# A four-layer network on one core: four changes of order, in two routers, an attention's projections and an attention's main loop

## The chip, the core and the metric

The kernel runs on one core of a Trainium2 chip. A core has TensorE (PE in the profile; its weight loads are PEld), VectorE (DVE), ScalarE (ACT), GpSimd (POOL) and SyncE (SP, which here only issues transfers). Every engine runs its own queue of instructions in order; an instruction that needs another engine's result waits at a semaphore, and all behind it on that queue wait too. The metric is device time in microseconds (us); the table below gives it for three runs.

## What is computed

Four layers, each of an attention or a recurrence and a feed-forward part, with a residual and a layer norm after each, on x of 4 x 512 tokens with 128 features, all in float32:

```python
x = _layernorm(x + _L0_attn_ref(x, ...))   # window attention
x = _layernorm(x + _L0_ffn_ref(x, ...))    # 16 experts, router r0
x = _layernorm(x + _L1_attn_ref(x, ...))   # direction attention, a1
x = _layernorm(x + _L1_ffn_ref(x, ...))    # 8 experts with capacity, router r1
x = _layernorm(x + _L2_attn_ref(x, ...))   # rotary attention, 8 heads of 128, a2
x = _layernorm(x + _L2_ffn_ref(x, ...))    # rotary attention, 16 heads of 64, h2; 31 experts
x = _layernorm(x + _L3_attn_ref(x, ...))   # recurrence
x = _layernorm(x + _L3_ffn_ref(x, ...))    # 8 experts, router r3 with a hidden layer
```

The four parts that the change touches compute this (shortened):

```python
# a1: three query and key numbers a head, and their products with fixed directions
q3 = (x @ Wq.T).reshape(B, T, 8, 3); k3 = (x @ Wk.T).reshape(B, T, 8, 3)
scores = einsum('bhtd,bhsd->bhts', q3, k3) * scale + q_on_dir[..., :, None] * k_on_dir[..., None, :]
# r1: the two best of 8 experts for each token; a place in the expert's list; then
h = gelu(einsum('ecd,edh->ech', exp_batches, c_fc)); exp_out = einsum('ech,ehd->ecd', h, c_proj)
# h2: on xn = _rmsnorm(x, gamma1), 16 heads of 64
q = _rope(xn @ q_w + q_b); k = _rope(xn @ k_w + k_b)
attn = softmax(where(causal, q @ k.T * scale, -inf)); attn_out = (attn @ v) @ o_w + o_b + xn
# r3
logits = gelu(xf @ gw1 + gb1) @ gw2 + gb2; scores = softmax(logits); topk_w, topk_idx = top_k(scores, 2)
```

## The kernel before

The program is a sequence of blocks, with a barrier of all engines between them. Activations lie feature-major: 128 features on the partitions, 2048 tokens along them, handled as four batches (B) of 512 columns (T). In every block each engine's order is written out by hand, and each wait names a semaphore and a count. A float32 matmul runs as two passes over its columns; where speed is wanted, operands are split into a rounded high part and a low part (value minus high part), and three single-pass products replace one.

**The norm at the head of a block** (Norm, lines 200 to 257, and Head, 259 to 320). For each batch b, PE centres the sum, ACT squares it, PE takes the variance, ACT makes the inverse root by Ln and Exp, and DVE multiplies (line 254), which gives x_fm. PE's order in Head.tensor is centre(b), variance(b - 1); behind the step b = 3 it calls the next part's tensor_early. Head.vector calls the next part's vector(dve, b) behind each of DVE's steps.

**Attention a1** (DirectionFront, 2427; direction_scores, 2045). The query and key weights (three rows a head) are spread to two 128 x 256 matrices by two products (line 2458, banks 0 and 1), copied to w_wide by DVE at b = 2 (line 2466), and at b = 3 the query part is multiplied by a scale (line 2472, which releases the semaphore scaled). PE waits for scaled, then runs 16 projections of 128 x 512 (line 2084) over four banks. Each result is split in three bfloat16 parts by ACT (2099, 2107), DVE (2134, 2146) and POOL.

**Router r1** (capacity_router, 1280) and its experts (capacity_experts, 1385). DVE ranks 8 logits a token, thresholds, counts (with two PE products, line 1324), and writes for each token and choice the row of its slot (slots, line 1382). Meanwhile ACT rounds the eight experts' first weights (w1_hi, line 1338) and POOL subtracts (w1_lo, line 1311). After the barrier POOL issues 32 indirect transfers (line 1415) that scatter the token rows to the experts' lists, SP fetches the lists, and PE starts the experts.

**Attention h2** (rope_attention with heads = 2, 1568). There are 32 units, one for a batch and a pair of heads. A unit U has four steps, one for each tile q of 128 queries, in the order q = 3, 0, 2, 1 (512, 128, 384 and 256 key columns, as the mask is causal). A step K has two items, one a head; item j = 2K + h uses score bank j % 5. The item's way: scores and mask on PE (lines 1739, 1742), the negative maximum on DVE (1932), the exponential with row sums on ACT (1852), transposes on PE into the same bank (1749), and a copy of these to p_t, by DVE for head 0 (1941) and by ACT for head 1 (1862). Scores of item j wait until the copy of item j - 5 has freed the bank. PE works one step ahead: scores(K + 1), transposes of K's head 0, a piece of other work, transposes of head 1, another piece; the pieces (function between) are the projections of unit U + 2 and the product with the values, the spread of the sums and the out product (line 1790) of unit U - 1. DVE runs maximum(K + 1), both heads, then copy_t(K). Rotary embedding of unit U + 2 goes through a swap of rows by SP's transfers and products on POOL. Attention a2 is the same function with heads = 1.

**Router r3** (router, 1017, with a hidden layer). PE computes two hidden tiles for each batch (line 1076, two banks in turn), ACT applies Gelu (1105), and behind all eight PE computes logits for 16 tiles of 128 tokens, two products each, which are 64 passes of 8 columns (line 1081). Then DVE ranks them. ACT rounds x (line 703) behind the last Gelu and POOL subtracts (x_lo, line 708).

## Time and profile before

| | us |
|---|---|
| median of three runs | 1852.05 (1846.07 to 1853.19) |
| the profiled execution | 1846.22, with a span of 1844.4 |
| mean granted clock of PE | 0.914 of full speed |

| engine | busy us | share of the span |
|---|---|---|
| PE | 1554.3 | 84% |
| PEld | 1002.0 | 54% |
| DVE | 1031.4 | 56% |
| ACT | 1004.5 | 54% |
| POOL | 767.2 | 42% |

The span is from the first to the last instruction; the profiled execution's time lies 1.8 us above it. A line of the page's groups gives busy time, mean time of one instruction and the idle time of its engine just before it. The idle times tell who waited, not whether it cost anything: ACT's exponentials in h2 stand idle before them for 132.4 us in all and DVE's maxima for 118.3, while PE's scores there show 20.6. Whether a wait counts must be read from the timeline of its stage. PE's clock is granted at one of two levels, 1.0 (2.4 GHz) or 0.5 (1.2 GHz); a number between is a mean over the stretch.

### The profile page before, as it was taken

How to read it: one execution, taken by the hardware profiler on the slowest of the kernel's cores; microseconds unless marked ns; L12 is line 12 of the kernel's file. 1: busy time of each engine (PE TensorE's matmuls, PEld its weight loads, DVE VectorE, ACT ScalarE, POOL GpSimd, SP SyncE). 2: the span in 40 equal slices, each digit the busy share in tenths (PEclk: the TensorE clock that was granted, in tenths of full speed). 3: DMA queues.
4: the chain of work that ended last, by engine and by line, in shares of the span. 5: the costliest groups of instructions: out<-in, count | busy, mean ns of one | idle time of the engine just before them, and what ended most of it. 6: DMA issues, size and time to landing. Idle time of an engine off the chain costs nothing. (4 is left out here: it accounts for less than half of the span.)

```text
span 1844.4 us, 27071 instructions
## 1 busy us (share of the span) xinstructions
PE 1554.3 (84%) x8739; PEld 1002.0 (54%) x8756; DVE 1031.4 (56%) x2126; ACT 1004.5 (54%) x2164; POOL 767.2 (42%) x712
## 2 busy tenths in 40 slices
PE   5658978860877899999789999999989999868898
PEld 3337643330874566666445555555448886323685
DVE  5956675631213655555355555555548886662575
ACT  4324554550423455555556656565538887664686
POOL 1224530027352566666264555545324443022263
PEclk8979977975887999999899999999979999979799
DMA  1008210021223222222211111111027652000330
GB/s 41 1 14 183 62 82 23 1 95 42 80 61 114 45 61 58 58 58 58 70 46 46 36 47 38 44 43 39 24 62 266 228 209 95 1 0 21 123 122 25
DMA packets 62165, 125.50 MB, mean 68 GB/s; under 512 B 14354, under 2 KB 29571, under 8 KB 55532
## 3 DMA queue, kind: packets, MB, share of 16 engines
q1 hardware_dynamic: 59724, 119.57, 22.2%
q0 software_dynamic: 2304, 4.24, 0.7%
q8 instruction: 69, 1.13, 0.3%
q14 instruction: 68, 0.56, 0.1%
HBM read 79.39 MB, written 11.35 MB: 49 GB/s over the span
## 5 line engine op out<-in xcount | busy, mean ns | idle before, releaser
L1852 ACT ACTIVATE h_probs<-psum,h_nmax 128x512 f32<-128x512 f32 (+3 forms) x256 | 132.7, 523 | 132.4 <-DVE h_nmax L1932 77.8
L1932 DVE TENSOR_REDUCE h_nmax<-psum 128x1 f32<-128x512 f32 (+3 forms) x256 | 113.5, 486 | 118.3 <-PE psum L1742 118.3
L1667 POOL TENSOR_TENSOR h_swapped<-h_swapped,rope_tables 128x512 f32<-128x512 f32 x64 | 81.9, 1280 | 158.4 <-DMA h_swapped<-h_raw 158.4
L897 ACT ACTIVATE psum<-psum,f_b 128x512 f32<-128x512 f32 x200 | 131.8, 659 | 27.8 <-PE psum L857 27.8
L823 POOL TENSOR_TENSOR e_lo<-e_gated,e_hi 128x512 fp32r<-128x512 f32 x59 | 76.1, 1290 | 148.1 <-ACT e_hi L909 148.1
L1852 ACT ACTIVATE a_probs<-psum,a_nmax 128x512 f32<-128x512 f32 (+3 forms) x128 | 67.6, 528 | 123.8 <-DVE a_nmax L1932 75.6
L1667 POOL TENSOR_TENSOR a_swapped<-a_swapped,a2f_a_tables 128x512 f32<-128x512 f32 x64 | 82.3, 1286 | 126.1 <-DMA a_swapped<-a_raw 125.9
L932 DVE TENSOR_TENSOR e_lo<-psum,e_hi 128x512 fp32r<-128x512 f32 x168 | 114.7, 683 | 26.4 <-ACT psum L897 26.4
L1739 PE MATMUL psum<-h_k,h_q 64*128 64x384 f32 (+3 forms) x512 | 104.9, 485 | 20.6 <-DVE h_p_t L1941 16.8
L855 PE MATMUL psum<-f_x_hi,f_w_hi 128*128 128x512 f32 x272 | 109.0, 401 | 5.8 <-DVE e_gated L946 3.9
L1749 PE MATMUL psum<-ident,h_probs 128*128 128x128 f32 x640 | 108.7, 277 | 0.4 <-ACT h_probs L1852 0.4
L856 PE MATMUL psum<-f_x_hi,f_w_lo 128*128 128x512 f32 x272 | 108.3, 398 | 0.0
L857 PE MATMUL psum<-f_x_lo,f_w_hi 128*128 128x512 f32 x272 | 108.1, 397 | 0.0
L1932 DVE TENSOR_REDUCE a_nmax<-psum 128x1 f32<-128x512 f32 (+3 forms) x128 | 62.4, 489 | 70.8 <-PE psum L1742 69.6
L1739 PE MATMUL psum<-a_k,a_q 128*128 128x512 f32 (+3 forms) x256 | 91.8, 441 | 6.4 <-DVE a_wvo L1924 6.4
L874 PE MATMUL psum<-e_lo,f_w_hi 128*128 128x512 f32 x236 | 92.8, 393 | 1.9 <-POOL e_lo L823 0.9
L871 PE MATMUL psum<-e_hi,f_w_hi 128*128 128x512 f32 x236 | 92.5, 392 | 0.0
L872 PE MATMUL psum<-e_hi,f_w_lo 128*128 128x512 f32 x236 | 92.4, 391 | 0.0
L1767 PE MATMUL psum<-h_p_t,h_v 128*64 128x256 f32 (+3 forms) x512 | 89.9, 451 | 0.0
L1739 PEld LDWEIGHTS psum<-h_k,h_q 64*128 64x128 f32 x512 | 40.0, 186 | 87.4 <-issue 49.4
L946 DVE TENSOR_TENSOR psum<-psum,e_gate 128x512 f32<-128x512 f32 x96 | 67.1, 699 | 33.4 <-ACT psum L897 29.0
L1749 PEld LDWEIGHTS psum<-ident,h_probs 128*128 128x128 f32 x640 | 72.0, 142 | 23.6 <-ACT h_probs L1852 19.2
(471 smaller groups left out, 4074.6 us busy)
## 6 DMA issues: line engine op xcount, KB each, us to landing
e_gate<-gates SPq DMA_DIRECT2D x39, 1024.0 KB, 4.8
a_swapped<-a_raw SPq DMA_DIRECT2D x128, 128.0 KB, 2.3
h_swapped<-h_raw SPq DMA_DIRECT2D x256, 64.0 KB, 2.0
e_gate<-gates SPq DMA_DIRECT2D x16, 512.0 KB, 7.4
f_w<-in_l_experts SPq DMA_DIRECT2D x17, 256.0 KB, 4.9
f_w<-in_l_experts SPq DMA_DIRECT2D x32, 128.0 KB, 4.7
slots<-a_empty SPq DMA_DIRECT2D x1, 2600.0 KB, 7.5
e_got<-slots SPq DMA_DIRECT2D x8, 325.0 KB, 5.5
```

The source lines that it names most:

```text
L855: nc.tensor.matmul(to, w_h, ex.x_hi[:, cols(b)], start=True, stop=False, skip_group_check=True)
L856: nc.tensor.matmul(to, w_l, ex.x_hi[:, cols(b)], start=False, stop=False, skip_group_check=True)
L857: nc.tensor.matmul(to, w_h, ex.x_lo[:, cols(b)], start=False, stop=True, skip_group_check=True).then_inc(hid_ready, 1)
L871: nc.tensor.matmul(to, w_h, hi[:, n % PLACES, :], start=start, stop=False, skip_group_check=True)
L874: nc.tensor.matmul(to, w_h, lo[:, n % PLACES, :], start=False, stop=True, skip_group_check=True).then_inc(out_done, 1)
L897: nc.scalar.activation(to, hidden_bank(n), ex.act_func, **bias(n)).then_inc(act_ready, 1)
L932: nc.vector.tensor_tensor(lo[:, n % PLACES, :], whole, hi[:, n % PLACES, :].bitcast(F32), ALU.subtract).then_inc(lo_dve, 1)
L1667: nc.gpsimd.tensor_tensor(swapped[:, j, :], swapped[:, j, :], tables[:, 2 * j + 1, :], ALU.mult).then_inc(sin_ready, 1)
L1739: nc.tensor.matmul(ring[j % RING][:, 0:(q + 1) * P], qs[rows, U % 3, q * P:(q + 1) * P], ks[rows, U % 3, 0:(q + 1) * P], start=True, stop= ...
L1749: last = nc.tensor.transpose(ring[j % RING][:, k * P:(k + 1) * P], probs[:, j % 4, k * P:(k + 1) * P], core.ident[:])
L1852: nc.scalar.activation(probs[:, j % 4, 0:(q + 1) * P], ring[j % RING][:, 0:(q + 1) * P], ACT.Exp, bias=nmax[:, j % 8:j % 8 + 1], accum_out ...
L1932: nc.vector.tensor_reduce(nmax[:, j % 8:j % 8 + 1], ring[j % RING][:, 0:(q + 1) * P], AX.X, ALU.max, negate=True).then_inc(max_ready, 1)
```

## The change

Four edits, none of which changes a value:

- r1: the low parts of the first weights are no longer subtracted by POOL in the router's block but by DVE at the start of the next block. PE waits for them (w1_split) before the first expert.
- r3: the logits of batch b - 1 are computed behind the hidden products of batch b; those of the last batch behind all.
- a1: tensor_early is called behind the step b = 1 of the norm on PE, and DVE's copies and scaling of the wide weights move from its steps 2 and 3 to its steps 0 and 1. Head is used by all blocks, but only a1 has a tensor_early.
- h2: at the last step of a unit (n = 3) DVE runs maximum(K + 1) for head 0, copy_t(K), then maximum(K + 1) for head 1. The end of the last unit, and a2, keep their order.

```diff
@@ Head.tensor
-            if b == B - 1:
+            if b == 1:
                 self.ahead.tensor_early(pe)
@@ router, tensor
+                def logits_of(b):
+                    pe.wait_ge(hid_ready, (b + 1) * KT)
+                    for t in range(b * QT, (b + 1) * QT):
+                        for k in range(KT):
+                            last = nc.tensor.matmul(logits[:, t, :], hid[:, k, t * P:(t + 1) * P], rw[:, k, :], start=k == 0, stop=k == KT - 1)
+                    return last
...
-                    pe.wait_ge(hid_ready, B * KT)
-                    for t in range(NT):
-                        for k in range(KT):
-                            last = nc.tensor.matmul(logits[:, t, :], hid[:, k, t * P:(t + 1) * P], rw[:, k, :], start=k == 0, stop=k == KT - 1)
-                    last.then_inc(logits_ready, 1)
+                        if b >= 1:
+                            logits_of(b - 1)
+                    logits_of(B - 1).then_inc(logits_ready, 1)
@@ capacity_router, gpsimd
-                for e in range(E):
-                    pool.wait_ge(w1_rounded, e + 1)
-                    nc.gpsimd.tensor_tensor(w1_lo[:, e, :], front.w1[:, e, :], w1_hi[:, e, :].bitcast(F32), ALU.subtract)
@@ capacity_experts, tensor
                 pe.wait_ge(front.w2_loaded, 16)
+                pe.wait_ge(w1_split, E)
@@ capacity_experts, vector
+                for e in range(E):
+                    nc.vector.tensor_tensor(w1_lo[:, e, :], front.w1[:, e, :], w1_hi[:, e, :].bitcast(F32), ALU.subtract).then_inc(w1_split, 1)
                 split_x(0)
@@ rope_attention, vector
-                def maximum(K):
+                def maximum(K, which=slice(None)):
...
-                    for j, h in step_items(K):
+                    for j, h in step_items(K)[which]:
...
-                    if K + 1 < steps:
+                    if K + 1 == steps:
+                        copy_t(K)
+                    elif heads == 2 and n == QT - 1:
+                        maximum(K + 1, slice(0, 1))
+                        copy_t(K)
+                        maximum(K + 1, slice(1, 2))
+                    else:
                         maximum(K + 1)
-                    copy_t(K)
+                        copy_t(K)
@@ DirectionFront.vector
-        if b == 2:
+        if b == 0:
...
-        if b == 3:
+        if b == 1:
```

DVE in h2, from the product that normalises a unit's values (h_y) on; h_nmax are the maxima, h_p_t the copies of transposed probabilities. Before:

```order
L1955 TENSOR_TENSOR h_y<-psum,h_r_sb 128x512
L1932 TENSOR_REDUCE h_nmax<-psum 128x1 x2
L1941 COPY h_p_t<-psum 128x2x128
L1932 TENSOR_REDUCE h_nmax<-psum 128x1 x2
L1941 COPY h_p_t<-psum 128x4x128
```

Now:

```order
L1960 TENSOR_TENSOR h_y<-psum,h_r_sb 128x512
L1937 TENSOR_REDUCE h_nmax<-psum 128x1
L1946 COPY h_p_t<-psum 128x2x128
L1937 TENSOR_REDUCE h_nmax<-psum 128x1 x3
L1946 COPY h_p_t<-psum 128x4x128
```

The copy of the last step (two tiles of 128) now stands between the two maxima of the next unit's first step; of the group of three, the first is the second head's and the other two belong to the step after.

PE at the start of a1, with the norm's centring (center_w) and variances (mean_w), the wide weights (a1w_spread) and the projections (a1w_w_wide). Before:

```order
L221 MATMUL psum<-sum_fm,center_w 128x512 x2
L241 MATMUL psum<-n0f__n0f_sq,mean_w 128x512
L221 MATMUL psum<-sum_fm,center_w 128x512
L241 MATMUL psum<-n0f__n0f_sq,mean_w 128x512
L221 MATMUL psum<-sum_fm,center_w 128x512
L241 MATMUL psum<-n0f__n0f_sq,mean_w 128x512
L2458 MATMUL psum<-a1w_spread,a1w_w 128x256 x2
L241 MATMUL psum<-n0f__n0f_sq,mean_w 128x512
L2084 MATMUL psum<-x_fm,a1w_w_wide 128x512 x4
```

Now:

```order
L221 MATMUL psum<-sum_fm,center_w 128x512 x2
L241 MATMUL psum<-n0f__n0f_sq,mean_w 128x512
L2469 MATMUL psum<-a1w_spread,a1w_w 128x256 x2
L221 MATMUL psum<-sum_fm,center_w 128x512
L241 MATMUL psum<-n0f__n0f_sq,mean_w 128x512
L221 MATMUL psum<-sum_fm,center_w 128x512
L241 MATMUL psum<-n0f__n0f_sq,mean_w 128x512 x2
L2095 MATMUL psum<-x_fm,a1w_w_wide 128x512 x4
```

The wide products moved from behind the third variance to behind the first, and nothing stands between the last variance and the projections.

PE in r3, with the hidden products (f_hw) and the logits (f_rw). Now (before it is one row of eight hidden products and one of 32 for the logits):

```order
L1083 MATMUL psum<-x_fm,f_hw 128x512 x4
L1071 MATMUL psum<-f_rw,r_hid 128x8 x8
L1083 MATMUL psum<-x_fm,f_hw 128x512 x2
L1071 MATMUL psum<-f_rw,r_hid 128x8 x8
L1083 MATMUL psum<-x_fm,f_hw 128x512 x2
L1071 MATMUL psum<-f_rw,r_hid 128x8 x16
```

Half of the logits now stand among the hidden products, half behind them.

## Rows read from the trace of the kernel before

**Rows 1.** Waits of 960 to 1320 us: waiter <- releaser: us, times, longest.
```profile
PE psum L1739 <- DVE h_p_t L1941: 12.8, 29, 0.4
```

**Rows 2.** Timeline in h2: start, length, engine, line, operation, count, [idle <-releaser].
```profile
1145.23 1.29 DVE L1932 TENSOR_REDUCE h_nmax<-psum 128x1 f32<-128x512 f32 x2 [0.26 <-PE psum L1742]
...
1145.53 1.02 PE L1790 MATMUL psum<-h_y,h2f_h_w 128*128 128x512 f32 x2
1146.01 0.69 ACT L1852 ACTIVATE h_probs<-psum,h_nmax 128x512 f32<-128x512 f32 x1 [1.82 <-issue]
1146.44 0.41 DVE L1941 COPY h_p_t<-psum 128x256 f32<-128x256 f32 x1
...
1147.00 0.49 PE L1739 MATMUL psum<-h_k,h_q 64*128 64x128 f32 x4 [0.44 <-DVE h_p_t L1941]
...
1147.54 0.61 PE L1749 MATMUL psum<-ident,h_probs 128*128 128x128 f32 x4
```

**Rows 3.** Timeline at the start of attention a1.
```profile
232.73 1.12 PE L2458 MATMUL psum<-a1w_spread,a1w_w 24*128 24x256 f32 x4
...
235.66 0.63 ACT L249 ACTIVATE n0f__n0f_rs<-n0f__n0f_rs 128x512 f32<-128x512 f32 x1
...
236.94 0.28 DVE L2472 TENSOR_SCALAR a1w_w_wide<-a1w_w_wide,a1w_scale 128x144 f32<-128x144 f32 x1
...
237.32 5.37 PE L2084 MATMUL psum<-x_fm,a1w_w_wide 128*128 128x512 f32 x8 [2.41 <-issue]
...
238.59 0.60 ACT L2099 ACTIVATE a1p_high<-psum 128x512 bf16<-128x512 f32 x1 [2.29 <-PE psum L2084]
...
243.42 3.60 PE L2084 MATMUL psum<-x_fm,a1w_w_wide 128*128 128x512 f32 x8
```

**Rows 4.** Groups by line and shape, 410 to 423 us: busy, mean ns, idle.
```profile
L1311 POOL TENSOR_TENSOR f_w_lo<-f_w,f_w_hi 128x512 fp32r<-128x512 f32 x8 | 10.1, 1300 | 1.4 <-ACT f_w_hi L1338 1.4
...
L1324 PE MATMUL psum<-r_chosen,f_counts 128*128 128x256 f32 x4 | 2.1, 674 | 6.7 <-DVE r_chosen L1363 6.7
...
L1379 DVE TENSOR_TENSOR r_upto<-r_upto,f_slot_base 128x256 f32<-128x256 f32 x1 | 1.4, 1367 | 0.0
L1363 DVE TENSOR_TENSOR r_chosen<-r_chosen 128x128 f32<-128x128 f32 x1 | 1.3, 1259 | 0.0
L1350 DVE TENSOR_SCALAR r_chosen<-r_marked 128x128 f32<-128x128 f32 x1 | 1.2, 1245 | 0.0
...
L1376 DVE SCALAR_TENSOR_TENSOR r_chosen<-r_upto,r_chosen 128x256 f32<-128x256 f32 x1 | 0.8, 833 | 0.0
L1380 DVE TENSOR_TENSOR r_upto<-r_upto,r_chosen 128x256 f32<-128x256 f32 x1 | 0.4, 424 | 0.0
```

**Rows 5.** Groups by line and shape in 422 to 467 us, the scatters.
```profile
L1415 POOL DMA_INDIRECT slots<-f_rows,f_slots x32 | 31.3, 980 | 12.0 <-issue 12.0
```

**Rows 6.** Line 1910: durations min/median/max ns, first and last start.
```profile
L1910 DVE TENSOR_TENSOR h_rot<-h_raw,rope_tables x32: 679/680/1662, 914.2 to 1307.0; 128x512 f32<-128x512 f32 x32
```

**Rows 7.** Timeline of router r3.
```profile
1695.04 5.89 PE L1076 MATMUL psum<-x_fm,f_hw 128*128 128x512 f32 x12 [1.81 <-ACT r_hid L1105]
...
1701.70 9.99 PE L1081 MATMUL psum<-f_rw,r_hid 128*128 128x8 f32 x64 [0.78 <-ACT r_hid L1105]
1702.25 4.95 POOL L708 TENSOR_TENSOR f_x_lo<-x_fm,f_x_hi 128x512 fp32r<-128x512 f32 x4 [7.96 <-ACT f_x_hi L703]
...
1711.80 0.29 DVE L1185 TENSOR_TENSOR r_scores<-psum,f_bias 128x128 f32<-128x128 f32 x1 [18.19 <-PE psum L1081]
...
1712.45 0.29 DVE L1187 TENSOR_TENSOR r_scores<-r_scores,r_small 128x128 f32<-128x128 f32 x1
```

**Rows 8.** Stretches: length, busy (count) PE PEld DVE ACT POOL, PEclk.
```profile
237.30:241.70 4.40, 4.38 (x7) 1.86 (x8) 1.58 (x3) 1.80 (x3) 0.00 (x0) 0.61 0.00 0
1701.70:1706.00 4.30, 4.30 (x39) 4.30 (x39) 0.00 (x0) 3.31 (x5) 3.75 (x4) 0.99 0.01 4
1706.00:1711.70 5.70, 5.69 (x28) 5.59 (x27) 0.00 (x0) 0.00 (x0) 1.19 (x1) 0.50 0.00 0
```

More of the change, by code:

```diff
@@ L1291, in capacity_router @@
         place = st.sb("place", [P, 2, NT])
-        (x_turned, first_rows, w1_rounded, shifted, exp_ready, chosen_ready, counted, dve_step) = (st.sem(n) for n in (
-            "x_turned", "first_rows", "w1_rounded", "shifted", "exp_ready", "chosen_ready", "counted", "dve_step"))
+        (x_turned, first_rows, shifted, exp_ready, chosen_ready, counted, dve_step) = (st.sem(n) for n in (
+            "x_turned", "first_rows", "shifted", "exp_ready", "chosen_ready", "counted", "dve_step"))
         within, totals = (core.psum[:, k, 0:2 * NT * E].rearrange("p (k t e) -> p k t e", k=2, e=E) for k in (1, 2))
@@ L1337, in _ @@
                     act.wait_ge(front.w1_loaded[e], 16)
-                    nc.scalar.activation(w1_hi[:, e, :], front.w1[:, e, :], ACT.Copy).then_inc(w1_rounded, 1)
+                    nc.scalar.activation(w1_hi[:, e, :], front.w1[:, e, :], ACT.Copy)
             @block.vector
@@ L1397, in capacity_experts @@
         hid = st.sb("hid", [P, 2, HT, CAPACITY])
-        (sent, turned, x_rounded, x_split, hid_psum, hid_ready, out_psum, out_ready, returned, joined) = (st.sem(n) for n in (
-            "sent", "turned", "x_rounded", "x_split", "hid_psum", "hid_ready", "out_psum", "out_ready", "returned", "joined"))
+        (w1_split, sent, turned, x_rounded, x_split, hid_psum, hid_ready, out_psum, out_ready, returned, joined) = (st.sem(n) for n in (
+            "w1_split", "sent", "turned", "x_rounded", "x_split", "hid_psum", "hid_ready", "out_psum", "out_ready", "returned", "joined"))
         got_loaded = [st.sem(f"got{e}_loaded") for e in range(E)]
```

## Prediction

> **What bounds the kernel now.** I read the page first: PE is busy 84% of the span, the other engines 42 to 56%, and the chain that ended last gives every line about 0%, so no single line bounds the program. Each stage has its own limit, and each edit must be priced in its own stage. I therefore read four stretches in the timeline: attention h2 (925 to 1341 us), the start of attention a1 (225 to 256), router r1 (393 to 468) and router r3 (1682 to 1723).
>
> In h2 a unit (one batch, two heads) takes about 12.9 us, 32 times, with PE nearly full. In the table of waits over 28 units the one true hole on PE is the 128-column scores waiting for DVE's copy of the transposed probabilities: 29 times, never over 0.4 us [rows 1]. The timeline shows its place. DVE starts the two 512-wide maxima at 1145.23, they take 1.29 us together, and only then, at 1146.44, comes the copy of step 3, head 0, which frees the bank that the next scores write. PE, whose last work was the two passes from 1145.53, starts those scores at 1147.00 [rows 2].
>
> In a1 PE builds the wide weights late, DVE scales them after the last norm step at 236.94, and PE's projections begin at 237.32; ACT's first split follows at 238.59 [rows 3]. In r1 DVE's small operations beside GpSimd's eight subtractions take up to 1.37 us where their like takes 0.42 [rows 4]. In r3 PE computes all hidden products first and then 64 passes for the logits in one block from 1701.70, and DVE waits for them until 1711.80 [rows 7]; in that block the granted clock is 0.99 (2.4 GHz) until 1706 and 0.50 (1.2 GHz) after [rows 8].
>
> **A copy between maxima (h2), the large term.** 31 times (the end of every unit but the last) DVE now runs max head 0, copy, max head 1. The two maxima take 1.29, so one occupies 0.65, and the copy can start near 1145.85 in place of 1146.44 and end near 1146.25; its transposes were issued ahead of 1145.53 and have ended. The scores started 0.15 after the copy's end, so they could now start at 1146.40. PE itself is free then: a 512-column fp32 pass takes its slot for 0.43 (eight of them 3.60, two 1.02, so (3.60 - 1.02)/6) [rows 2, 3], and two from 1145.53 end their slots at 1146.39. The gap between 1146.39 and 1147.00 is 0.61; the profile calls 0.44 of it a wait [rows 1, 2]. Some 0.1 between unlike groups of matmuls will stay, so I take 0.50: 31 x 0.50 = 15.5 us. The ends are 31 x 0.44 = 13.6 and 31 x 0.61 = 18.9.
>
> What is late next? PE's own order is scores, mask, transposes of head 0 at 1147.54, so 1147.0 after the change. They need the exponential that starts at 1146.01 and that the change does not move; with 0.69 for it and 0.1 for its accumulator it is done at 1146.8, 0.2 ahead [rows 2]. The second maximum is late by the copy's step, 0.41 less the usual overlap, about 0.33. The second exponential, bound by it, then ends near 1147.7; its transposes stand behind a projection of three passes and are wanted near 1148.2. ACT's copy behind it is also 0.3 later, in time for a bank that is reused over 1 us later. So the cost of 0.33 is covered by about 0.4 us, a thin cover, and it is paid in full if that is gone. POOL and the swap transfers work two units ahead and I charge nothing for them.
>
> **Wide weights in the norm's second step (a1).** The two products move from behind the third variance to behind the first. They take 1.12 us [rows 3] and PE is full there, so norm steps 1 to 3 move later; the last variance, held up by them today, then waits for its square instead. Walking the norm through ACT's order, the last exponential moves from 235.66 to about 236.0. Against that, DVE no longer scales after the last step, and PE goes from the last variance straight to the projections, at about 235.1 in place of 237.32. ACT's first split can start when its last exponential (0.63) is over, 236.75 in place of 238.59: 1.8 us gained. Today PE idles before it begins and gets a clock of 0.61 on average there [rows 8], so the first eight passes take 5.37 us, and eight a little later 3.60 [rows 3]. Without the hole the clock should stay at its upper level, which frees up to 1.8 us on PE; ACT, next in line and busy itself, lets through perhaps a third, 0.6. Sum 2.4, with ends 0 (another engine holds the stage) and 1.8 + 1.8 = 3.6 us. The weights' loads are issued by 226.7 and would have to land after 229.2 to add a wait.
>
> **Low parts off GpSimd (r1).** The eight subtractions leave POOL (10.1 us). Of DVE's operations beside them, the threshold L1350 falls from 1.25 to 0.29-0.42, the difference L1363 from 1.26 to 0.29 (the like in r3), L1376 from 0.83 to 0.42 and L1379 from 1.37 to 0.42 [rows 4, 7]: 0.9 + 1.0 + 0.4 + 0.9 = 3.2 us. L1365 and L1367 are slowed as well, but PE's two counting products (2.1 us) run beside them and DVE waits for these, so nothing comes of that. Slots, barrier and the 32 scatters move up by 3.2. The eight subtractions now stand first on DVE in the next block, ahead of split_x(0): 8 x 0.68 = 5.4 us by the 128x512 row with two SBUF operands [rows 6]. 32 scatters with 31.3 us of work and 12.0 of idle ahead of them hide them [rows 5], and PE's new wait for them is over long before the first gathered rows. What they do to POOL's scatters no row shows: at least 0; at most all of their 5.4. The nearest row: under DVE's interference POOL's eight subtractions still averaged 1.30 [rows 4], so POOL loses little and I take 0.5. Net gain 2.7, ends 3.2 and -2.2.
>
> The rule that speaks against this edit is in the Trainium skill, SBUF — State Buffer, section Who interferes with whom: a DVE instruction with two SBUF inputs contends with a GpSimd instruction that reads SBUF, and the second to issue blocks fully, but not with one that only writes. By that page the scatters, which read their offsets and data addresses, might be held for the whole of DVE's subtractions; the sum would then be 4.9 us worse, which is the fourth rival. No run here shows it.
>
> **Logits among the first products (r3).** Hidden products n2 to n7 run from 1695.04, each two passes of 0.43: 12 x 0.43 = 5.2 us. In the full-clock window 39 logits passes take 4.30 us, 0.11 each; in the half-clock one, 28 take 5.70, 0.20 each [rows 8]. Interleaved, PE has no hole: products of a batch, then the logits of the one before, whose Gelu is over by then. Ends: 1695.04 + 5.2 + 64 x 0.11 = 1707.3, if the clock stays up because full products stand between (the block began at full clock and kept it for over 4 us). DVE's first router operation was at 1711.80, 0.1 behind PE; it comes 4.4 us sooner. But Gelu ends 3 us later, so ACT's rounding and POOL's four x_lo subtractions (4.95) move from 1702.25 to about 1705.2-1710.2, now beside DVE's start. L1187 and L1191, with two SBUF operands, each wait for a POOL instruction: up to 1.0 together. Gain 3.5. The ends: at today's mean of 9.99/64 = 0.156 a pass it would be 1.5 - 1.0 = 0.5; without any blocking 4.4.
>
> **Sum.** 15.5 + 2.4 + 2.7 + 3.5 = 24.1 us. Against the profiled execution's own 1846.2 that is 1822.1. The median of the runs shown is 5.8 us above the profiled one, and I forecast a median: 1852.05 - 24.1 = 1828.
>
> **Rivals.** (1) h2 keeps half of its hole: the transposes of head 0 have only 0.2 us of margin, and semaphore latencies could eat 0.25 a unit. 24.1 - 7.8 = 16.3, 1836. (2) h2 gains nothing: the hole on PE appears elsewhere in the unit, since DVE's maxima mostly wait for PE's mask and ACT for DVE, a loop whose length the copy may not set. For it: these waits are there in the timeline; against: both engines wait because PE is late, and PE itself never stands long. Then 8.6 us, 1843.5. (3) Slower: DVE's queue becomes the loop. The copy waits for its transposes, and maximum head 1, its exponential and the transposes of head 1 queue behind that wait. It decides if the transposes end after 1146.6 instead of before 1146.0; the price is then about the whole copy and latencies, 1.0 a unit, +31 - 8.6 = +22 us, 1874. The order on PE speaks against it. (4) The scatters are held by DVE's subtractions: 4.9 worse, 1833.
>
> **How the numbers follow.** Forecast 0.62; rivals (1) 0.10, (2) 0.12, (3) 0.05, (4) 0.11. The bounds of the terms alone give gains from 11.9 (13.6 + 0 - 2.2 + 0.5) to 30.1 (18.9 + 3.6 + 3.2 + 4.4), that is 1840 to 1822 from the median; a measured median may also fall to the lowest of the runs shown, 6 us below, so the low end is 1816. The high end takes in rival (2): 1844. A measurement tells about 0.5% (9.3 us) from no change: below 1842.8 is faster. The forecast and rivals (1) and (4) lie there; rival (2) lies at the border, some of it on either side. Faster 0.84, same 0.11, slower 0.05.
>
> **What would show it.** h2: the 128-column scores start 0.1 us after PE's out product, no DVE wait ahead of them, and the unit is 12.4 us long; wrong if it is still 12.9. a1: first projection directly behind the last variance with clock 1.0, first split at 236.8. r1: first scatter 3.2 us sooner, then spacing as before; wrong if the first four are spread by 5 us. r3: logits passes of 0.11 throughout and DVE's start 4.4 us sooner. The forecast fails mainly if the h2 unit's length is not set by PE's queue.

## The result and the profile after

The changed kernel takes 1823.10 us (median of six runs, 1820.54 to 1829.45); the kernel before took 1852.24 on the same occasion. The ratio is 0.985, 95% interval 0.983 to 0.987, a gain of 28 us (25 to 31). The forecast was 1828, 24.1 us below the median of before. The profiled execution of the changed kernel took 1824.96 with a span of 1823.2. Its page gives each engine's busy time, share and instructions:

```profile
PE 1552.0 (85%) x8756; PEld 999.4 (55%) x8756; DVE 1033.2 (57%) x2134; ACT 1005.3 (55%) x2164; POOL 758.9 (42%) x704
```

PE is as busy as before within 2.3 us; what went is idle time between its products. GpSimd has 8.3 us less to do, and the eight subtractions take 4.9 us on DVE.

The span fell by only 21 us, since the profiled execution of before lies at the fast end of its kernel (1846.07 to 1853.78). One pair of profiles is therefore a poor witness for small terms: stages that no edit touches differ by up to 5 us between them (from h2's last maximum to the next norm 227.5 us before and 232.1 after). I use the pair for the mechanisms and all fourteen profiles of this study for the sizes (the table below).

**Attention h2.** The timeline of the changed kernel at the end of a unit (start, length, engine, line, operation, [idle before <- releaser]); it answers to [rows 2]:

```profile
1118.25 0.69 DVE L1937 TENSOR_REDUCE h_nmax<-psum 128x1 f32<-128x512 f32 x1 [0.27 <-PE psum L1747]
1118.85 0.41 DVE L1946 COPY h_p_t<-psum 128x256 f32<-128x256 f32 x1
1119.18 0.68 DVE L1937 TENSOR_REDUCE h_nmax<-psum 128x1 f32<-128x512 f32 x1
...
1119.02 0.69 ACT L1857 ACTIVATE h_probs<-psum,h_nmax 128x512 f32<-128x512 f32 x1 [1.82 <-issue]
...
1118.55 1.02 PE L1795 MATMUL psum<-h_y,h2f_h_w 128*128 128x512 f32 x2
1119.50 0.49 PE L1744 MATMUL psum<-h_k,h_q 64*128 64x128 f32 x4
...
1120.05 0.61 PE L1754 MATMUL psum<-ident,h_probs 128*128 128x128 f32 x4
```

The copy stands between the maxima. The scores follow PE's out product by 0.95 us from start to start, with no idle time recorded ahead of them; before it was 1.47 (1145.53 to 1147.00). The copy is over at 1119.26, 0.24 us before they start, so they no longer wait for it. In 950 to 1310 us the table of waits has no row for PE at all, where it had 12.8 us [rows 1], and the page's group of the scores shows what is left of their idle time, 7.5 us where before it was 20.6:

```profile
L1744 PE MATMUL psum<-h_k,h_q 64*128 64x384 f32 (+3 forms) x512 | 104.9, 486 | 7.5 <-POOL h_k L1677 5.0
```

From the first maximum of one unit to that of the next it is 12.38 us in 29 of the 31 spacings, where it was 12.90.

**Attention a1.** The start of the stage, whose first product begins at 227.61 (225.15 before); it answers to [rows 3], and the stretch under it to [rows 8] (length; busy and count of PE, PEld, DVE, ACT, POOL; granted clock; DMA share, GB/s):

```profile
236.77 1.12 PE L241 MATMUL psum<-n0f__n0f_sq,mean_w 128*128 128x512 f32 x2 [0.21 <-ACT n0f__n0f_sq L233]
...
237.33 0.63 ACT L249 ACTIVATE n0f__n0f_rs<-n0f__n0f_rs 128x512 f32<-128x512 f32 x1
...
237.74 3.60 PE L2095 MATMUL psum<-x_fm,a1w_w_wide 128*128 128x512 f32 x8
...
239.20 1.07 ACT L2110 ACTIVATE a1p_high<-psum 128x512 bf16<-128x512 f32 x2
```

```profile
235.00:240.00 5.00, 4.79 (x12) 1.94 (x11) 2.26 (x5) 4.90 (x9) 0.00 (x0) 1.00 0.00 0
```

The projections stand directly behind the last variance and run at 2.4 GHz, 3.60 us for eight passes in place of 5.37. Counted from the stage's first product, ACT's first split comes at 11.6 us in place of 13.4 (239.20 - 227.61; 238.59 - 225.15).

**Router r1.** Groups by line in 399 to 412 us (busy, mean ns | idle before), which answer to [rows 4], and the timeline of GpSimd behind them, to [rows 5]:

```profile
L1326 PE MATMUL psum<-r_chosen,f_counts 128*128 128x256 f32 x4 | 2.1, 674 | 5.7 <-DVE r_chosen L1365 5.7
...
L1373 DVE TENSOR_TENSOR_SCAN r_upto<-f_counts,psum 128x32 f32<-128x32 f32 x8 | 1.0, 200 | 1.6 <-PE psum L1326 1.6
...
L1378 DVE SCALAR_TENSOR_TENSOR r_chosen<-r_upto,r_chosen 128x256 f32<-128x256 f32 x1 | 0.4, 426 | 0.0
...
L1381 DVE TENSOR_TENSOR r_upto<-r_upto,f_slot_base 128x256 f32<-128x256 f32 x1 | 0.4, 425 | 0.0
...
L1365 DVE TENSOR_TENSOR r_chosen<-r_chosen 128x128 f32<-128x128 f32 x1 | 0.3, 293 | 0.0
```

```profile
412.03 1.53 POOL L1417 DMA_INDIRECT slots<-f_rows,f_slots  x1 [11.56 <-issue]
413.87 1.29 POOL L1417 DMA_INDIRECT slots<-f_rows,f_slots  x1 [0.30 <-issue]
415.47 1.50 POOL L1417 DMA_INDIRECT slots<-f_rows,f_slots  x1 [0.30 <-issue]
417.27 0.98 POOL L1417 DMA_INDIRECT slots<-f_rows,f_slots  x1 [0.30 <-issue]
```

The blocked operations are back at 0.29 and 0.42, and DVE now waits 1.6 us for PE's counts. The first three scatters, the only ones that overlap with DVE's eight subtractions, are slower than the 0.97 of the rest. Where nothing runs beside them the first takes 1.18 (shown with the additions below), so they lose (1.53 - 1.18) + (1.29 - 0.97) + (1.50 - 0.97) = 1.2 us.

**Router r3.** PE, GpSimd and DVE in the timeline; they answer to [rows 7]:

```profile
1677.24 1.96 PE L1083 MATMUL psum<-x_fm,f_hw 128*128 128x512 f32 x4 [1.81 <-ACT r_hid L1110]
1679.03 1.85 PE L1071 MATMUL psum<-f_rw,r_hid 128*128 128x8 f32 x16
...
1684.23 1.96 PE L1083 MATMUL psum<-x_fm,f_hw 128*128 128x512 f32 x4
1686.04 3.63 PE L1071 MATMUL psum<-f_rw,r_hid 128*128 128x8 f32 x32
...
1687.52 4.99 POOL L708 TENSOR_TENSOR f_x_lo<-x_fm,f_x_hi 128x512 fp32r<-128x512 f32 x4 [10.80 <-ACT f_x_hi L703]
...
1689.78 0.29 DVE L1190 TENSOR_TENSOR r_scores<-psum,f_bias 128x128 f32<-128x128 f32 x1 [13.97 <-PE psum L1071]
1690.11 0.29 DVE L1191 TENSOR_REDUCE r_small<-r_scores 128x16 f32<-128x128 f32 x1
1690.43 0.95 DVE L1192 TENSOR_TENSOR r_scores<-r_scores,r_small 128x128 f32<-128x128 f32 x1
```

Each pass of the logits takes 0.11 us (1.85/16, 3.63/32), at 2.4 GHz throughout; the clock falls 1.8 us behind the last. That is no wide margin: in the changed kernel's second profile it fell 0.8 us before the logits ended (in the kernel with the subtractions late 0.7), and without r1's edit 2.3 us before, which made this stretch 0.3 and 1.0 us longer. From n2's start (1677.24, 1695.04 before) to DVE's start is 12.5 us in place of 16.8. One of DVE's operations, L1192, is blocked by GpSimd for 0.66 us.

**Sizes from fourteen profiles.** Each column is a stretch between first starts of named instructions, in us: A from the norm's first square in a1 to the one of the next stage; B from that square to the first a_nmax; C in r1 from the copy of the logits to the slots; D from the first to the last of the 32 scatters; E from PE's first product on gathered rows until its granted clock rises to 2.4 GHz (to 0.5 us); F from the first to the last h_nmax; G from the norm's first square in r3 to that of the last norm.

| kernel | A | B | C | D | E | F | G |
|---|---|---|---|---|---|---|---|
| before | 163.9 | 43.2 | 17.5 | 39.8 | 6.0 | 404.3 | 144.7 |
| h2 alone | 164.0 | 43.3 | 16.8 | 39.7 | 6.0 | 387.2 | 144.3 |
| a1 alone | 156.2 | 40.0 | 16.4 | 39.8 | 7.0 | 403.3 | 144.8 |
| r1 alone | 163.9 | 43.2 | 14.1 | 41.0 | 8.5 | 405.6 | 143.2 |
| r3 alone | 164.0 | 43.3 | 16.9 | 39.8 | 6.0 | 405.4 | 141.2 |
| changed | 156.3 | 40.1 | 13.9 | 41.1 | 8.0 | 387.2 | 141.1 |
| changed, again | 163.8 | 41.4 | 14.1 | 40.9 | 8.0 | 389.7 | 141.2 |
| changed, copy first | 160.8 | 40.2 | 14.1 | 41.0 | 8.0 | 402.8 | 141.1 |
| changed, projections late | 160.4 | 43.7 | 14.1 | 40.9 | 7.5 | 389.3 | 141.1 |
| changed without r1 | 156.3 | 40.2 | 16.4 | 39.7 | 6.5 | 388.7 | 140.4 |
| changed without a1 | 163.9 | 43.2 | 14.0 | 41.0 | 7.5 | 389.1 | 141.1 |
| changed, subtractions late | 160.9 | 40.2 | 14.1 | 39.8 | 5.5 | 387.2 | 141.2 |
| changed, rounding early | 156.2 | 40.1 | 13.9 | 41.0 | 8.0 | 389.0 | 140.8 |
| both additions | 156.2 | 40.0 | 13.9 | 39.8 | 5.5 | 389.3 | 140.8 |

### The profile page after: what moved, and what is told of

The parts are those of the page before. It is cut to its first block and busy times, and to the rows that moved or that the text cites. A ratio compares the mean times of both kernels' runs of the same rounds, so it can differ in the third digit from the quotient of the medians.

```text
span 1823.2 us, 27092 instructions
## 1 busy us (share of the span) xinstructions
PE 1552.0 (85%) x8756; PEld 999.4 (55%) x8756; DVE 1033.2 (57%) x2134; ACT 1005.3 (55%) x2164; POOL 758.9 (42%) x704
## 5 line engine op out<-in xcount | busy, mean ns | idle before, releaser
L897 ACT ACTIVATE psum<-psum,f_b 128x512 f32<-128x512 f32 x200 | 131.8, 659 | 27.4 <-PE psum L857 27.3
L1772 PE MATMUL psum<-a_p_t,a_v 128*128 128x512 f32 (+3 forms) x256 | 82.4, 444 | 0.0
```

The costliest lines, as they stand in the source:

```text
L897: nc.scalar.activation(to, hidden_bank(n), ex.act_func, **bias(n)).then_inc(act_ready, 1)
L1772: last = nc.tensor.matmul(misc[1][d, k * P:T], stationary, p_t[:, U % 2, h, k, k * P:T], start=k == 0, stop=k == QT - 1, skip_group_check= ...
```

## The experiments

### Each edit alone

Four kernels, each the kernel before with one part of the diff above, timed together on one chip beside the kernel before (1853.21).

**The copy between the maxima.**

> The kernel before with the copy between the two maxima alone. Theory (rows 1 and 2): the unit of the long run of units falls from 12.90 to 12.38 us, as in the changed kernel, and first to last h_nmax gets 15 to 17 us shorter; the time falls by 15.5 to 17 us, a ratio of about 0.991. Rival: the whole of the 29 us of the changed kernel is here (ratio 0.984), the other edits giving nothing. Rival: the other edits make it possible (their share is over half), ratio above 0.995.

Measured: 1831.86 us, ratio 0.989 (0.986 to 0.992), a gain of 21 us (15 to 27), against the 15.5 to 17 expected. The durations (min/median/max ns) with first and last start of the maxima, in before and then in this kernel:

```profile
L1932 DVE TENSOR_REDUCE h_nmax<-psum x256: 278/486/693, 927.4 to 1331.7; 128x1 f32<-128x512 f32 x32, 128x1 f32<-128x128 f32 x32, 128x1 f32<-128x384 f32 x32, 128x1 f32<-128x256 f32 x32
```

```profile
L1932 DVE TENSOR_REDUCE h_nmax<-psum x256: 278/486/692, 927.5 to 1314.7; 128x1 f32<-128x512 f32 x32, 128x1 f32<-128x128 f32 x32, 128x1 f32<-128x384 f32 x32, 128x1 f32<-128x256 f32 x32
```

404.3 us became 387.2, and the unit is 12.38 us long as in the changed kernel. Over the table, column F has a mean of 404.7 in the four kernels without the edit and 388.5 in the nine with it (the one with the copy first left out): 16.1 us, 0.52 for each of 31 units. The edit is by far the largest of the four, and it needs none of the others.

**The wide weights early.**

> The kernel before with the wide weights of the first stage made in step 2 of the norm alone. Theory A, only the order: the first split of ACT starts 1.8 us earlier and the time falls by 2 to 3 us. Theory B, the clock: the weight-less hole of TensorE ahead of the first projections is gone, and the granted clock rises earlier in the direction attention as well, as in the profile of the changed kernel (half speed until 285 instead of 299 us), so that the first attention is 7 us shorter; the time falls by 6 to 9 us. Rival: the earlier rise is chance, and doesn't show again here.

Measured: 1849.88 us, ratio 0.997 (0.995 to 0.999), 5.6 us (2.0 to 8.9). Column A is 156.2 in place of 163.9: 3.2 us are there at the first maxima (B), and 4.5 come later, with a clock that rises earlier (4.1 of them between the first and the third a_nmax). The interval of the timing holds both theories. The profile agreed with theory B; the next runs show that this was half luck.

**The low parts on DVE.**

> The kernel before with the low parts of the weights on VectorE alone. Theory (rows 4 to 7): the router's small VectorE operations give back 3.2 us, the first three or four scatters cost GpSimd 1.2 us more as in the profile of the changed kernel; the time falls by 2.0 to 2.8 us. Rival: the scatters are held for the whole of the eight subtractions (4.9 us), and the time rises by about 1.7 us.

Measured: 1846.45 us, ratio 0.996 (0.994 to 0.998), 7.2 us (4.1 to 10.4). The profile has column C 14.1 in place of 17.5 and D 41.0 in place of 39.8, so the scatters are not held for the eight subtractions. It does not account for 7 us; see below. The execution that was profiled took 1850.37 us, 3.9 above this kernel's median.

**The logits among the products.**

> The kernel before with the logits of the last router among the first products alone. Theory: the first maximum comes 3.5 us earlier, and the time falls by 3 to 3.6 us. Rival: the logits products between the hidden products delay ACT's Gelus by as much as they save behind them; the time stays within 1 us of the kernel before.

Measured: 1850.54 us, ratio 0.999 (0.997 to 1.001): 2.6 us with 0 inside its interval. Column G settles it: 143.2 to 144.8 in the four profiles without the edit, 140.4 to 141.2 in the ten with it, a difference of the means of 3.2 us.

### The changed kernel again

> The changed kernel once more, timed on the chip of the next three. Theory (four edits add up): 1823 to 1828 us, a ratio to the kernel before of 0.983 to 0.987; the first direction attention again 7.7 us shorter with the clock at half speed for some 24 us of it and not 39, since two kernels with the edit of the first stage and four without it fell into these two cases. If the clock's early rise is chance, this stretch is as long as in the kernel before in this profile or another.

Measured: 1822.51 us, ratio 0.984 (0.981 to 0.987). This is at the lower end of the 1823 to 1828 expected, and the gain repeats. What does not is the early clock in a1. The stretch 286 to 296 us in the changed kernel, and in the same kernel again:

```profile
286.00:296.00 10.00, 8.36 (x102) 4.20 (x103) 7.30 (x18) 5.36 (x9) 0.00 (x0) 1.00 0.01 2
```

```profile
286.00:296.00 10.00, 9.91 (x79) 4.93 (x71) 5.81 (x13) 3.18 (x6) 0.00 (x0) 0.50 0.01 2
```

102 passes at 2.4 GHz against 79 at 1.2 GHz: the same kernel falls into either case. Theory B as written, that the edit brings the early rise each time, is wrong.

### The copy ahead of both maxima

```diff
-                        maximum(K + 1, slice(0, 1))
                         copy_t(K)
-                        maximum(K + 1, slice(1, 2))
+                        maximum(K + 1)
```

> The changed kernel with the copy of a unit's last step ahead of both maxima. The first maximum and the exp that it releases start 0.4 us later, the scores after the copy 0.6 us earlier than in the changed kernel if they could. Theory (the out product sets the scores now, rows 2; the first exp has 0.2 us to spare): scores no earlier, first exp 0.2 us over its margin, so that a unit takes 12.4 to 12.6 us and the time is 0 to 6 us above the changed kernel. Rival (the copy still sets the scores): a unit below 12.3 us and the time 3 us or more below it.

Measured: 1839.61 us, ratio 0.993 (0.990 to 0.995), 17 us above the changed kernel of the same occasion. Both expectations were wrong: nearly all of the edit's gain is gone, column F is 402.8 against 404.7 without the edit, and the unit is 12.85 us long. Timeline of this kernel at the same place, and its waits of PE in 950 to 1310 us (total, times, longest):

```profile
1142.97 0.42 DVE L1946 COPY h_p_t<-psum 128x256 f32<-128x256 f32 x1 [0.55 <-PE psum L1754]
1143.31 1.81 DVE L1937 TENSOR_REDUCE h_nmax<-psum 128x1 f32<-128x512 f32 x4
...
1144.07 0.69 ACT L1857 ACTIVATE h_probs<-psum,h_nmax 128x512 f32<-128x512 f32 x1 [2.43 <-issue]
...
1142.99 1.02 PE L1795 MATMUL psum<-h_y,h2f_h_w 128*128 128x512 f32 x2
1143.94 0.49 PE L1744 MATMUL psum<-h_k,h_q 64*128 64x128 f32 x4
...
1144.90 0.33 PE L1754 MATMUL psum<-ident,h_probs 128*128 128x128 f32 x1 [0.25 <-ACT h_probs L1857]
```

```profile
PE psum L1754 <- ACT h_probs L1857: 7.2, 28, 0.3
```

The scores again follow the out product by 0.95 us, so a still earlier copy buys nothing: PE's own queue sets them. The copy now waits 0.55 us for its transposes and the maxima queue behind that wait. Counted from the start of the out product, the first exponential is at 1.08 us, in the changed kernel at 0.47: 0.61 later. The transposes behind it are at 1.91 in place of 1.50, 0.41 later. So 0.2 us of the move was covered, the margin of the prediction, and the rest was paid 31 times (12.85 - 12.38 = 0.47 a unit). My expectation had counted the copy's own time and forgotten its wait. This is rival (3) made real, in milder form: 0.47 a unit and not 1.0. Both chains have 0.2 us to spare at this place, PE's scores behind the copy and the first exponential ahead of its transposes, and of the three places that were timed the one between the maxima suits both.

### Projections held back in a1

```diff
                 pe.wait_ge(head.ahead.scaled, 1)
+                head.wait(pe, B - 1)
```

> The changed kernel with TensorE waiting for all four variances before the first projection, so that the idle stretch of TensorE ahead of the projections (rows 3, 8) is back, the wide weights staying where the change puts them. Theory A (order): ACT's first split returns to 13.4 us after the norm's start, 1.8 us later than in the changed kernel, and the whole costs 2 to 3 us. Theory B (clock): the clock's early rise in the direction attention is lost as well, this stretch takes 164 us again and the whole costs 7.7 us. Rival: TensorE's later start is hidden behind ACT's own exps, less than 1 us.

The wait is for the last normalised batch and not, as the expectation says, for the last variance; the hole is 2.37 us long, as before (2.41). Measured: 1825.42 us, ratio 0.985 (0.982 to 0.988), 1.9 us above the changed kernel by the ratios, inside their intervals. PE in the timeline:

```profile
235.11 1.13 PE L241 MATMUL psum<-n0f__n0f_sq,mean_w 128*128 128x512 f32 x2 [0.21 <-ACT n0f__n0f_sq L233]
238.60 3.67 PE L2096 MATMUL psum<-x_fm,a1w_w_wide 128*128 128x512 f32 x8 [2.37 <-DVE x_fm L254]
```

ACT's first split comes 15.2 us after the stage's first product, not the 13.4 of theory A. Column B is 43.7, 3.5 us above its usual 40.1 to 40.2. Some 1.3 of them lie ahead of the hole: the norm's last variance ended as late as in the changed kernel's second profile (B 41.4), where the clock was low for longer at the norm's start. The other 2.3 are the price of holding PE, most of the order gain of the edit.

Two things about the clock can be read here. The eight passes take 3.67 us, so they run at full clock right behind a hole as long as the one of before: the missing hole is not shown to be what gives the projections their full clock in the changed kernel. And the clock rose early: A less B is 116.7, as in the changed kernel's first profile (116.2) and not as in before (120.7). So the order gain and the clock are separate, and a hole ahead of the projections does not rule out the early rise. This is one profile.

### The changed kernel without a1, without r1

Each is the changed kernel with one part of the diff undone.

> The changed kernel without the edit of the first stage. Theory: the first maxima of the direction attention come 43.2 us after the norm's start and not 40.1 (3.1 us), and the clock rises 29 us after them, as in the four kernels so far without this edit, where it rose after 15 us in four and after 29 us in two of the six with it; an early rise is worth 4.1 us. The time is 3 to 6 us above the changed kernel. Rival: early or late rise is the same chance with and without the edit; then this profile or another without the edit shows it after 15 us, and the time is 3 us above.

Measured: 1830.12 us, ratio 0.988 (0.985 to 0.990). Of the three kernels of the same occasion that have the edit, two stand at 0.985, and the third, with an addition that is shown below, at 0.981. By the first two the edit is worth some 4 us, in the range expected, but the intervals overlap. Columns A and B are 163.9 and 43.2, the late case again.

The count for a1 is now: late rise in five profiles of five without the edit, early in five and late in three of eight with it (the kernel with held projections left out). In every one the clock is low behind the projections, and rises about 15 or about 29 us after the first a_nmax. An early rise is worth 4.1 us between the first and third a_nmax. So the edit is worth 3.1 us at the first maxima (43.2 to 40.1; one profile of the eight has 41.4), and a chance at 4 more; the mean of A is 163.9 without and 158.3 with it, 5.6 us. Whether the edit shifts the odds is not settled by the count: none of five against five of eight could be luck, about one time in twenty. The traces say a little more. The clock fell 11.6 to 11.7 us ahead of the first a_nmax in all five profiles without the edit and 11.89 to 12.01 us ahead in seven of the eight with it, and among these the five in which it fell 11.91 us ahead or more are the early ones, the two at 11.89 and 11.90 late ones; the eighth, at 10.6, is late too. (With the projections held it fell 9.3 us ahead, and the rise was early.) So the case seems to hang on where PE's work lies against the moments at which the clock changes, which the edit moves to the border between the cases. This is a reading of the rows and was not tested, and why there are two places is open.

> The changed kernel without the edit of the first router: the low parts are GpSimd's again, under the router's small operations. Three terms were read from ten profiles: VectorE's operations from the copy of the logits to the slots take 16.8 us with GpSimd's subtractions beside them and 13.9 without (2.9), the first scatters are 1.2 us faster without VectorE's subtractions beside them, and the granted clock rose 5.5 to 7.0 us after the first product of the experts in the five kernels without eight subtractions right behind the slots and 7.5 to 8.5 us in the five with them (1.0). Theory: the edit is worth 2.9 - 1.2 - 1.0 = 0.7 us, so that this kernel is 0 to 2 us above the changed one and the clock rises within 7 us of the first product. Rival: the 7 us that the timing of this edit alone gave (3 to 10) are real, and lie somewhere that no profile was read for.

Measured: 1823.73 us, ratio 0.985 (0.983 to 0.988), against 0.985 and 0.984 of the changed kernel on two other occasions: no difference that the timing tells, as the theory said. Timeline of DVE, with GpSimd's subtractions beside it again:

```profile
404.60 1.25 DVE L1368 TENSOR_TENSOR r_chosen<-r_chosen 128x128 f32<-128x128 f32 x1
...
410.96 1.37 DVE L1384 TENSOR_TENSOR r_upto<-r_upto,f_slot_base 128x256 f32<-128x256 f32 x1
```

The columns give r1's terms. C falls from a mean of 16.8 (five profiles) to 14.0 (nine), 2.8 us. D rises from 39.8 to 41.0 in each of the seven with the eight subtractions beside the scatters, 1.2 us. And E is 5.5 to 7.0 in the seven profiles without them there and 7.5 to 8.5 in the seven with. The stretch from 5.0 to 7.5 us behind the first product, here and in the changed kernel:

```profile
464.50:467.00 2.50, 2.50 (x15) 2.50 (x14) 0.56 (x2) 1.79 (x5) 0.00 (x0) 0.66 0.34 131
```

```profile
463.30:465.80 2.50, 2.50 (x12) 2.50 (x11) 0.59 (x2) 1.69 (x4) 0.00 (x0) 0.50 0.37 144
```

Counted from the first product the rise is 1.9 us later by the means, and costs about half of that, since the passes take twice the time at 1.2 GHz. The sum is 2.8 - 1.2 - 0.9 = 0.7 us.

It would be wrong to say that the subtractions delay the clock. Take this kernel and the changed one: the copy of the logits is at 396.9 and 396.8, the first product at 459.5 and 458.3, and the rise at 466.2 and 466.1. The product came 1.2 us sooner, the rise did not move. In twelve of the fourteen profiles, with the subtractions and without, the rise comes 68.8 to 69.6 us after the copy of the logits, wherever between 61.2 and 63.8 us the first product lies. The other two are those with the subtractions late, described next; their first product is at 60.1 and 60.4 us, and the rise at 65.8 and 66.1. So the rise stays while the product moves, until it falls into an earlier place. What sets these places is open. So is the difference to the 7.2 us of this edit alone: its interval ends at 4.1, and neither its profile nor this kernel shows a place for as much.

### Two additions

The first: DVE starts the eight subtractions when 31 of the 32 scatters have landed, instead of beside the first ones.

```diff
+                dve.wait_ge(sent, (2 * NT - 1) * 16)
                 for e in range(E):
                     nc.vector.tensor_tensor(w1_lo[:, e, :], ...)
```

The last scatter has a semaphore of its own (last_sent), for which SyncE waits as well.

> The changed kernel with the eight subtractions of the first router started when 31 of 32 scatters have landed, alone. Theory: scatters 1.2 us faster, the clock rises within 7 us of the first expert product (1.0), in all 2.2 us below the changed kernel. Rival: the subtractions hold up the first expert's low part, so that the first product is 0.5 us or more later.

Measured: 1816.05 us (1815.28 to 1818.29), ratio 0.981 (0.979 to 0.983). GpSimd's first scatters, and DVE:

```profile
418.91 1.18 POOL L1417 DMA_INDIRECT slots<-f_rows,f_slots  x1 [10.58 <-issue]
420.39 0.97 POOL L1417 DMA_INDIRECT slots<-f_rows,f_slots  x1 [0.30 <-issue]
```

```profile
459.80 4.91 DVE L1533 TENSOR_TENSOR f_w_lo<-f_w,f_w_hi 128x512 fp32r<-128x512 f32 x8 [42.01 <-DMA slots<-f_rows,f_slots]
465.36 0.89 DVE L1524 TENSOR_TENSOR e_x_lo<-psum,e_x_hi 128x384 fp32r<-128x384 f32 x2 [0.65 <-ACT e_x_hi L1502]
```

D is 39.8 again and E 5.5, and the subtractions end 0.65 us before DVE is wanted. The rival is refuted, both terms of the theory are there: 2.2 us. (The second is the earlier place of the rise, not a delay that went.) The timing gives about 6 (0.981 against 0.984 and 0.985 on other occasions), more than the profile accounts for; the intervals leave room for 2.

The second: in r3 ACT rounds batch 0 behind its Gelus, batches 1 and 2 behind those of batch 1, batch 3 behind those of batch 2.

> The changed kernel with ACT's rounding of each batch behind that batch's Gelus in the last stage, alone. Theory: GpSimd's four subtractions end before VectorE's router operations begin, the blocked one (0.95 us) takes 0.29 again, 0.7 us below the changed kernel, less than the timing can tell, so that the profile decides. Rival: the rounding between the Gelus delays the hidden part of the next batch and the logits; the maximum comes 0.5 to 1.5 us later.

Measured: 1822.75 us, ratio 0.985 (0.983 to 0.988). GpSimd's last subtraction is over before DVE begins, and the blocked operation takes its 0.29:

```profile
1676.35 1.26 POOL L708 TENSOR_TENSOR f_x_lo<-x_fm,f_x_hi 128x512 fp32r<-128x512 f32 x1 [1.01 <-ACT f_x_hi L703]
...
1682.12 0.29 DVE L1195 TENSOR_TENSOR r_scores<-psum,f_bias 128x128 f32<-128x128 f32 x1 [13.97 <-PE psum L1071]
...
1682.77 0.29 DVE L1197 TENSOR_TENSOR r_scores<-r_scores,r_small 128x128 f32<-128x128 f32 x1
1683.43 0.29 DVE L1199 TENSOR_REDUCE r_small<-r_scores 128x16 f32<-128x128 f32 x1 [0.38 <-ACT r_scores L1124]
```

From the norm's first square to the first of DVE's maxima for the ranking is 25.25 us in place of 25.93, the 0.7 expected, and the rival is refuted. The timing can't tell it.

Both together:

> The changed kernel with two additions. The eight subtractions of the low parts start when 31 of the 32 scatters have landed (the last scatter has a semaphore of its own), so that GpSimd's first scatters go at their 0.97 us again: 1.2 us. In the last stage ACT rounds each batch's hidden part behind that batch's Gelus, so that GpSimd's subtractions are over before VectorE's block of small operations: 0.7 us. Theory: both hold, the time is 1.9 us below the changed kernel. Rival: the subtractions are late for the first expert product (5 us of VectorE from the landing of the 31st on), which costs 1 to 3 us and leaves the time as it is or above.

Measured: 1816.98 us (1814.19 to 1820.60), ratio 0.980 (0.978 to 0.983); the changed kernel of the same occasion has 0.984. By the profile the additions are worth 2.9 us (the 1.9 expected left out the clock), by the ratios some 6, with intervals that overlap. The rival, a late first product, is refuted. This is, with the first addition alone, the fastest version of the study, some 6 us below the changed kernel and 35 to 37 below the kernel before.

## Why the prediction held, point by point

- **h2, 15.5 us (13.6 to 18.9): right, the size too.** 16.1 over all profiles, 0.52 a unit where 0.50 stood. The scores start with PE's out product, the unit is 12.38 us long where 12.4 was the sign, and the margin named for the first exponential, 0.2 us, is as thin as it was said to be: the kernel with the copy first overran it and lost nearly everything. No run tests the 0.4 us of cover for the second. Rival (1) had argued from that thinness; the place between the maxima does not touch it. Rival (2) did not come, because PE's hole was filled and none opened elsewhere. Rival (3) did not come, because the copy is never reached before its transposes are done.
- **a1, 2.4 us (0 to 3.6): order right, the clock's share too small.** The step that failed is "lets through perhaps a third, 0.6". ACT's first split came 1.8 us sooner, as worked out, and 3.1 us of gain reach the first maxima, so 1.3 of the 1.8 that the full clock frees came through. That the missing hole keeps the clock up is not shown: with the hole back the projections ran at full clock too. The clock's rise later in the stage, worth 4.1 us when it falls early, was not in the prediction at all; the mean is 5.6.
- **r1, 2.7 us (-2.2 to 3.2): the first half right, the second mis-sized.** DVE's operations gave 2.8 where 3.2 stood. The term that was too large is the threshold's 0.9: the 1.25 us was in the profile of before alone, and the same operation took 0.24 to 0.69 in the other four kernels with GpSimd's subtractions beside it. The other three delays (1.0, 0.4 and 0.9) went as priced, and the 1.6 us that DVE now waits for PE's counts stands where before's L1365 and L1367 were slowed, from which the prediction rightly took nothing. The scatters lost 1.2 where 0.5 was taken, and about 0.9 is lost again because the clock's rise did not come forward with the first product, which no term had. About 0.7 us is left, if the profiles are right and not the 7.2 (4.1 to 10.4) that this edit's own timing gave. Rival (4) is refuted by column D. The rule of the Trainium skill (SBUF — State Buffer, Who interferes with whom) that stood behind it holds at most in part here: subtractions with two SBUF operands did slow the three scatters beside them, by 1.2 us in all, but did not hold them for their 4.9 us. For arithmetic on both engines the trace agrees with it: DVE's difference with two SBUF operands went from 1.26 to 0.29 when GpSimd's subtractions left. But so did an operation that reads a single tensor (before's L1365, 128x16, from 1.23 to 0.17), which the rule as the prediction gives it does not cover.
- **r3, 3.5 us (0.5 to 4.4): right.** 3.2. The clock stayed up through the logits, 0.11 a pass, in seven of the ten profiles with the edit, DVE began 4.3 us sooner where 4.4 was set, and one DVE operation was blocked for 0.66 us, where up to 1.0 was set.
- **The sum.** The prediction had 24.1, the terms as measured make 16.1 + 5.6 + 0.7 + 3.2 = 25.6, and the timing says 28 (25 to 31). The step from the profiled execution to the median was right to take: before has 1852 to 1854 in each of its sets of runs. What the sum lacks against the measured 28 is inside its interval. That 24.1 lies so near to 25.6 is partly luck: a1 was 3.2 too low and r1 2.0 too high, and most of a1's error is the later clock, which stood in no term.

The four edits timed alone make 36 us together, against 28 for all at once. Their intervals are 3 to 6 us wide on either side, and the profiles add up, so I read no interaction into it. Nor is a small one excluded: the difference of 8 us is about as wide as the five intervals taken together.

## What to carry to other kernels

In a loop in which one engine is nearly full, look for the one instruction whose release it waits for and move that ahead by as little as frees it; moving it further can push a chain that has only some tenths of a microsecond to spare, and then the loss is as large as the gain was. A queued instruction costs its own wait as well as its own length to all behind it. Terms of a few microseconds should be read as stretches between named instructions over several profiles, since the clock moves whole stages by 4 us and more between executions of one kernel (column A of the changed kernel: 156.3 and 163.8).

## What the runs showed of the hardware

- TensorE's granted clock falls into one of two cases at the same place of the same kernel: in the direction attention it rose about 15 or about 29 us after the first a_nmax, and from the first to the third a_nmax it is 27.3 to 27.4 us in the first case and 31.4 to 31.8 in the second. Two profiles of the changed kernel show one each.
- After 50 to 52 us without products, the clock rose 5.5 to 8.5 us after the first product. The rise did not follow the product: in twelve profiles it came 68.8 to 69.6 us after the copy of the logits while the first product lay at 61.2 to 63.8, and in the two with the product at 60.1 and 60.4 it came at 65.8 and 66.1.
- With 512-column products between them, the 64 passes of the logits took 0.11 us each at 2.4 GHz; in one block they took 0.11 until the clock fell, some 4.3 us in, and 0.20 from there. In three of the ten profiles with the edit the clock fell 0.7 to 2.3 us before the last logits all the same.
- GpSimd's indirect scatters beside DVE's 128x512 subtractions with two SBUF operands took 1.53, 1.29 and 1.50 us in place of 1.18, 0.97 and 0.97; each is held for a part. The other 29 start after the subtractions have ended.
